# Correcting the diagonal block of the second attention by one addition of a skewed product, with four score banks

## What is computed

```
r     = sinusoid(S-1 ... 0, dk)                       # position vectors
term1 = einsum('bhqd,bhkd->bhqk', Q, K)
term2 = einsum('bhqd,kd->bhqk', Q, r)
term3 = einsum('hd,bhkd->bhk', u, K)
term4 = einsum('hd,kd->hk', v, r)
scores = (term1 + term3 + rel_shift(term2 + term4)) / sqrt(dk)
attn  = softmax(scores)
```

## Time and profile before

| | us |
|---|---|
| median of 3 timed runs | 2261.0 (2257.3 to 2263.5) |
| profiled execution | 2253.5 |
| its span, first to last instruction | 2251.5 |
| TensorE busy in the span | 1776.5 (79%) |
| VectorE busy | 1507.1 (67%) |
| ScalarE busy | 1508.9 (67%) |
| first attention | about 137 to 970 |
| mixing | about 980 to 1152 |
| second attention | about 1153 to 1905 |
| dense | about 1905 to 2251 |

### The profile page before, as it was taken

How to read it: one execution, slowest core, us unless ns; L and a number is a source line. 1 busy time by engine, 2 the same in 40 slices (tenths; PEclk the granted TensorE clock), 3 DMA queues, 4 the chain that set the end, 5 groups by cost and what they waited for, 6 DMA issues and landing times. The chain is left out here.

```text
span 2251.5 us, 44817 instructions
## 1 busy us (share of the span) xinstructions
PE 1776.5 (79%) x12182; PEld 1060.1 (47%) x12182; DVE 1507.1 (67%) x3898; ACT 1508.9 (67%) x2584; POOL 71.3 (3%) x102
## 2 busy tenths in 40 slices
PE   2407999999899989838628888888888885899998
PEld 1204555555555555525415444554454553444554
DVE  2636888888888888828848777777777774342431
ACT  2306888888888888828838788888778885222322
POOL 0000000000000000004400000000000000000000
PEclk9657999999999999969959999999999998899999
DMA  3947889889899889736852222222222221210000
GB/s 91 378 168 227 265 261 269 263 264 269 254 272 266 259 256 271 239 101 184 288 176 77 65 66 70 66 67 63 67 68 68 65 70 46 68 37 19 23 19 10
DMA packets 319461, 340.71 MB, mean 151 GB/s; under 512 B 24960, under 2 KB 241128, under 8 KB 319232
## 3 DMA queue, kind: packets, MB, share of 16 engines
q1 hardware_dynamic: 319360, 339.67, 49.7%
HBM read 193.23 MB, written 146.37 MB: 151 GB/s over the span
## 5 line engine op out<-in xcount | busy, mean ns | idle before, releaser
L750 ACT ACTIVATE a_prob<-bank,a_negmax 128x512 f32<-128x512 f32 x1024 | 712.8, 696 | 107.2 <-DVE a_negmax L695 97.2
L695 DVE TENSOR_REDUCE a_negmax<-bank 128x1 f32<-128x512 f32 x1024 | 700.0, 684 | 0.1
L757 ACT COPY a_probt<-bank 128x512 f32<-128x512 f32 x1024 | 597.9, 584 | 142.1 <-PE bank L587 128.8
L587 PE MATMUL bank<-a_ident,a_prob 128*128 128x128 f32 x4096 | 649.8, 282 | 34.8 <-ACT a_probt L757 31.2
L587 PEld LDWEIGHTS bank<-a_ident,a_prob 128*128 128x128 f32 x4096 | 439.5, 143 | 93.7 <-ACT a_probt L757 51.8
L672 DVE COPY_PREDICATED bank<-a_mask,bank 128x128 f32<-128x128 uint32 (+1 forms) x1024 | 290.0, 283 | 257.9 <-PE bank L572 169.5
L563 PE MATMUL bank<-a_stks 65*128 65x192 bf16 (+7 forms) x1024 | 327.9, 320 | 165.0 <-ACT a_prob L750 114.6
L563 PEld LDWEIGHTS bank<-a_stks 65*128 65x128 bf16 (+1 forms) x1024 | 100.1, 98 | 445.7 <-ACT a_prob L750 392.6
L600 PE MATMUL bank<-a_probt,a_vs 128*32 128x512 f32 x2048 | 275.5, 612 | 1.7 <-ACT a_probt L757 1.7
L569 PE MATMUL bank<-a_stks 96*128 96x128 bf16 (+2 forms) x1024 | 225.9, 221 | 33.6 <-DVE bank L672 23.3
L682 DVE TENSOR_TENSOR bank<-bank,a_band 128x192 f32<-128x192 f32 (+1 forms) x512 | 200.2, 391 | 59.1 <-DMA a_band<-shear_b 58.5
(11 more groups left out here) (165 smaller groups left out, 1541.8 us busy)
## 6 DMA issues: line engine op xcount, KB each, us to landing
a_band<-shear_b SPq DMA_DIRECT2D x128, 512.0 KB, 5.3
shear_a<-a_keyside SPq DMA_DIRECT2D x128, 256.0 KB, 4.5
a_sheared<-shear_a SPq DMA_DIRECT2D x128, 256.0 KB, 4.7
shear_b<-a_corr SPq DMA_DIRECT2D x128, 256.0 KB, 5.1
a_stks<-stack SPq DMA_DIRECT2D x128, 192.0 KB
a_stks<-stack SPq DMA_DIRECT2D x256, 96.0 KB
heads_out<-a_outs SPq DMA_DIRECT2D x64, 256.0 KB, 2.2
stack<-part SPq DMA_DIRECT2D x16, 768.0 KB, 5.2
```

The lines of the kernel that those rows point to most:

```text
L587: last = pe.transpose(turned_bank[k][:, n * 128:(n + 1) * 128], prob[h.slot % 2][:, n, k * 128:(k + 1) * 128], ident[:, :])
L695: v.tensor_reduce(negmax[h.slot % 2][:, n:n + 1], score[:, :], AX.X, ALU.max, negate=True).then_inc(maxed, 1)
L750: nc.scalar.activation(prob[h.slot % 2][:, n, :], score[:, :], ACT.Exp, bias=negmax[h.slot % 2][:, n:n + 1]).then_inc(exped, 1)
L757: nc.scalar.copy(probt[h.slot][:, k, :], turned_bank[k][:, :]).then_inc(copied, 1)
```

## The change

In the second attention the score tile is now cut at column 128n + 129: near product to the left, far product to the right, both into one of four score banks. The masked copies and their products go. Instead, what row q lacks from column q + 1 on inside the block (minus its own near product, plus the next query's product, and zero in column q + 1) depends on the column's distance to the diagonal alone, so it is a product of an unrotated query array with a fixed matrix of 96 rows and 128 columns (`edges`). TensorE makes it per head (`edge`), VectorE copies it out (`edge_out`), SyncE writes it to `shear_b` and reads it back skewed, as in the first attention, and `finish` adds it. Lookahead becomes 7 and 5 tiles. The stack gets a fifth array (the query with v, unrotated), which the mixing stage splits and writes too. The dense stage's code loses the parts that only layer 0 would have used; its instructions stay.

```diff
+KEY, EDGE, NEAR, FAR = range(4)
+ARRAYS = 5
-SCORE_AHEAD, EXP_AHEAD = 6, 4
+SCORE_AHEAD, EXP_AHEAD = {0: 6, 1: 7}, {0: 4, 1: 5}
...
-                score_banks = bank[0:4] if rel else bank[0:3]
-                others = bank[4:5] if rel else bank[3:5]
+                score_banks = bank[0:4]
+                other = bank[4]
-                key_bank, corr_bank = bank[5], bank[6]
+                key_bank, corr_bank = bank[5], bank[6] if rel else bank[4]
...
-                        sp.dma_start(stk[j][0:SR, KLO:QLO + 1, :], stack[1][b, :, own, 0:2, :]).then_inc(stk_in[j], 16)
-                        sp.dma_start(stk[j][0:SR, KHI, :], stack[1][b, :, own, 0, :]).then_inc(stk_in[j], 16)
-                        sp.dma_start(stk[j][0:SR, QHI, :], stack[1][b, :, own, 1, :]).then_inc(stk_in[j], 16)
-                        sp.dma_start(stk[j][SR:R1, QLO:QHI + 1, :], stack[1][b, :, own, 2:4, :]).then_inc(stk_in[j], 16)
+                        sp.dma_start(stk[j][0:SR, KEY:NEAR + 1, :], stack[1][b, :, own, 0:3, :]).then_inc(stk_in[j], 16)
+                        sp.dma_start(stk[j][0:SR, FAR, :], stack[1][b, :, own, 2, :]).then_inc(stk_in[j], 16)
+                        flat = stack[1][b, :, own, :, :].rearrange("j c a t -> j c (a t)")
+                        sp.dma_start(stk[j][SR:R1, EDGE, :], flat[:, :, T + 1:2 * T + 1]).then_inc(stk_in[j], 16)
+                        sp.dma_start(stk[j][SR:R1, NEAR:FAR + 1, :], stack[1][b, :, own, 3:5, :]).then_inc(stk_in[j], 16)
...
-                    if rel and left > 1:
+                    if left > 1:
                         hold(sp, added, 4 * (n + 1))
                         shear_b_read(sp, Head(i, j + 2))
-                    if rel and left > 2:
+                    if left > 2:
                         shear_b_write(sp, Head(i, j + 3))
...
                         for j in range(1 if rel else 0, LOAD_AHEAD):
                             head_load(sp, Head(0, j))
+                        if not rel:
+                            sp.wait_ge(edges_set, BASE + 3)
+                            sp.dma_start(edges[SR:R1, :], back[:, :]).then_inc(edge_in, 16)
+                            every = bass.AP(t["poskey"].tensor, 0, [[T, SR], [0, unroll], [1, T]])
+                            sp.dma_start(stks[SR:R1, :, KEY, :], every).then_inc(poskey_in, 16)
+                            for j in range(2):
+                                shear_b_write(sp, Head(0, j))
+                                shear_b_read(sp, Head(0, j))
+                            shear_b_write(sp, Head(0, 2))
...
+                    def edge(pe, h):
+
+                        pe.wait_ge(corr_copied, BASE + h.n)
+                        pe.wait_ge(stk_in[h.slot], BASE + per_stk * (h.i + 1))
+                        for n in range(NT):
+                            q = slice(128 * n, 128 * n + 128)
+                            last = pe.matmul(corr_bank[:, q], stk[h.slot][:, EDGE, q], edges[:, :], start=True, stop=True)
+                        last.then_inc(corr_mm, 1)
...
+                            if not rel and k == 1 and left >= CORR_AHEAD:
+                                edge(pe, Head(i, j + CORR_AHEAD))
...
                         if not rel:
+                            pe.wait_ge(edge_in, BASE + 48)
+                            for j in range(CORR_AHEAD):
+                                edge(pe, Head(0, j))
...
+                    def edge_out(v, h):
+                        v.wait_ge(corr_mm, BASE + h.n + 1)
+                        v.wait_ge(b_written, BASE + 16 * (h.n - 1))
+                        v.tensor_copy(corr[h.slot % 2][:, :, :], corr_bank[:, :].rearrange("p (n r) -> p n r", n=NT)).then_inc(corr_copied, 1)
...
+                                if left >= (k + score_ahead) // NT:
+                                    if rel:
+                                        mix(v, *ahead(i, j, k, score_ahead))
+                                    else:
+                                        finish(v, *ahead(i, j, k, score_ahead))
+                                if left >= (k + score_ahead - 1) // NT:
+                                    row_max(v, *ahead(i, j, k, score_ahead - 1))
...
+                                if not rel and k == 3 and left >= CORR_AHEAD:
+                                    edge_out(v, Head(i, j + CORR_AHEAD))
...
-                HALF = 2 * T
+                WIDE = 5 * T + 2
+                QV, KEYS, QU, ROT0, ROT1 = 0, T + 2, 2 * T + 2, 3 * T + 2, 4 * T + 2
+                HALVES = slice(0, ROT0), slice(ROT0, WIDE)
-                N_STACK = 4 * len(TERM_RUNS)
+                N_STACK = ARRAYS * len(TERM_RUNS)
```

More of the change, by code:

```diff
@@ L352, in attention_phase @@
                 ident = sb("ident", [128, 128])
-                mask = sb("mask", [128, 128], U32)
                 outs = sb("outs", [128, T])
+                wide = WIN if rel else REL
+                corr = [sb(f"corr{i}", [128, NT, REL]) for i in range(2)]
+                band = [sb(f"band{i}", [128, NT, wide]) for i in range(2)]
+                if not rel:
+                    edges, signs = sb("edges", [R1, REL], BF16), sb("signs", [SR, 2])
+                    waves, back = sb("waves", [SR, T], BF16), sb("back", [SR, REL], BF16)
                 if rel:
+                    mask = sb("mask", [128, 128], U32)
                     tabs = sb("tabs", [RF, unroll, 2 * REL], BF16)
@@ L709, in _ @@
                         else:
-                            for j in range(unroll):
-                                v.memset(stks[0:R1, j, KHI, :], 0.0).then_inc(blank, 1)
+                            v.memset(back[:, 0:1], 0.0).then_inc(edges_set, 1)
+                            v.wait_ge(edge_in, BASE + 32)
+                            v.tensor_copy(back[:, 1:REL], bass.AP(waves[:, :].tensor, T - 1, [[T, SR], [-1, REL - 1]])).then_inc(edges_set, 1)
+                            v.tensor_scalar(edges[0:SR, :], waves[:, 1:REL + 1], signs[:, 0:1], -1.0, ALU.mult, ALU.mult).then_inc(edges_set, 1)
@@ L721, in _ @@
+                        for n in range(score_ahead):
+                            if rel:
+                                mix(v, *ahead(0, 0, 0, n))
+                            if rel and n:
                                 row_max(v, *ahead(0, 0, 0, n - 1))
                             finish(v, *ahead(0, 0, 0, n))
+                            if not rel and n:
+                                row_max(v, *ahead(0, 0, 0, n - 1))
                         def vector_step(i, j, left):
                             for k in range(NT):
-                                if left >= (k + SCORE_AHEAD) // NT:
-                                    mix(v, *ahead(i, j, k, SCORE_AHEAD))
@@ L774, in _ @@
                                 corr_out(act, Head(0, j))
-                        for n in range(EXP_AHEAD):
+                        for n in range(exp_ahead):
                             exp_tile(act, *ahead(0, 0, 0, n))
@@ L1485, in gated_products, with flip @@
+                            last.then_inc(e["out_mm"], 1)
+                        def flip(b):
+                            pe.wait_ge(e["x1"], BASE + b + 1)
+                            for n in range(NT):
+                                last = pe.transpose(flip_bank[:, n * 128:(n + 1) * 128], x1n[:, n, :], ident[:, :])
+                            last.then_inc(e["tr1"], 1)
                         def gated_products(b):
@@ L1714, in step1, with step @@
-                        def step1(b, more, load):
+                            v.wait_ge(e["x1"], BASE + b + 1)
+                            v.tensor_copy(x1[:, :, :], x1n[:, :, :]).then_inc(e["kept"], 1)
+                            v.wait_ge(e["kept"], BASE + b + 1)
+                        def step(b, more, load):
                             for m in range(KH):
@@ L1726, in step1 @@
                                 keep_rows1(b + 1)
-                            rows2(b)
-                        if first:
-                            v.memset(xt1[:, 0:1], 0.0).then_inc(fill, 1)
-                            v.memset(vt[:, :, :, DH:VC], 1.0).then_inc(fill, 1)
-                            for i in range(3):
-                                v.memset(part[:, i, 4 * T:4 * T + 2], 0.0).then_inc(fill, 1)
-                            v.wait_ge(fill, BASE + 5)
+                            v.wait_ge(e["f_stored"], BASE + 16 * b)
+                            rows(v, b, pre2, x2, 2)
                         v.wait_ge(c_in, BASE + 16 * N_FIRST)
@@ L1740, in _ @@
                         keep_rows1(0)
-                        if first:
-                            token_mix(0)
-                            relu(0)
-                            residual2(0)
-                            rows2(0)
-                        steps(v, step0 if first else step1)
+                        steps(v, step)
         tables_phase()
@@ L1755, in build @@
         end_phase()
-        dense_phase(1)
+        dense_phase()
 def _tables(np):
```

450 lines of the change are left out of this document (127 added, 323 removed).

## The result

The changed kernel takes 2387.3 us (median of 4 runs, 2378.1 to 2392.3) against 2261.3 (2257.3 to 2263.5) for the kernel before: a ratio of 1.056, 95% interval 1.052 to 1.059. It is 126 us slower, and 104 us above the forecast. The profiled execution has a span of 2385.7 us against 2251.5, 134 us more.

The account below looks back on a forecast made before the run. SyncE's issues and the band's round trip were taken to bound the changed second attention. Loop -4, start +23, last heads -5 and mixing +12 gave +26 us, so 2283 us (base 2257), range 2238 to 2320.

Parts of the forecast that it names:

- the circle: Second attention's loop: band read landing, VectorE's steps, next write, loads, next read; two heads need L + 7.9, 5.78 us a head.
- L: Second attention: time for the 256 KB band read to land, taken as 3.0 us.
- the stall at the loop's edge: Second attention's 12-head loop: 0.38 us a head before; claimed to fall mostly into time VectorE waits anyway.
- SyncE becomes the bound and eats the gain: Second attention's loop: added DMA issues make it 5.70 us a head against 5.74, -4 us instead of 155 gained.
- SyncE alone 5.53: Second attention's loop: SyncE's issues alone take 5.53 us a head, 5.3 to 5.7 depending on the gap.
- rival (c): Second attention's loop: the circle binds harder, L = 3.6 or more, 6.0 to 6.1 us a head, about 2320 us; chance 0.13.
- Start +23: Start of the second attention: edge load stands behind seven heads' loads, first exponential 23 us later (18 to 28).
- Last heads -5: Last 16 heads, outside the second attention's loop: 81 us against 86, -5 (-12 to +3).
- Mixing +12: Mixing stage: splitting and writing a fifth array adds 12 us (8 to 20), 8.4 of it splitting.
- Rival (a): Second attention's loop: SyncE does not set the pace; ScalarE does, 4.7 us a head with leftovers, 2170 us; chance 0.15.
- Rival (d): Score banks, second attention: bank change does nothing since TensorE stays late; same time as forecast; chance within the forecast's 0.50.
- the signs named: Second attention's profile: SyncE hardly waiting for group output, VectorE waiting for most band reads, weighting products 5.5 to 5.8 us apart.

Follow-up runs that it names:

- early: Changed kernel with VectorE's band-product copy moved ahead of the band-read wait and TensorE's product one tile step earlier: 2340.2 us, 1.037 of the kernel before.
- pool: Changed kernel with the four stack loads of each head in the second attention issued by GpSimd instead of SyncE: 2318.6 us, 1.027 of the kernel before.
- unroll8: Changed kernel with 8 instead of 12 heads in the loop body of the second attention: 2353.6 us, 1.044 of the kernel before.
- shift: Changed kernel with 64 small semaphore instructions on SyncE in front of the second attention's loop, body unchanged: 2346.9 us, 1.038 of the kernel before.
- mix4: Changed kernel with four of five arrays stored in the mixing stage, splitting still over five, loads reading another array: 2325.3 us, 1.030 of the kernel before.
- noband: Changed kernel without the band product's store and read in the second attention's loop, compute kept: 2144.0 us, 0.950 of the kernel before.
- before_shift: Kernel before, with 64 small semaphore instructions on VectorE in front of the second attention's loop: 2221.8 us, 0.985 of the kernel before.
- nohold: Changed kernel without the 12 small semaphore instructions behind SyncE's waits in the second attention's loop body: 2375.4 us, 1.052 of the kernel before.
- load24: Changed kernel with the last of four stack loads reading arrays 2 and 3 instead of 3 and 4: 2380.7 us, 1.055 of the kernel before.
- pool_ring: `pool_early2` with four band-product buffers, a semaphore per scratch place, and SyncE's store ahead of the same step's read: 2297.5 us, 1.017 of the kernel before.
- pool_early2: Changed kernel with loads on GpSimd, band copy ahead of the band wait, TensorE's product right behind the first score tile: 2246.9 us, 0.996 of the kernel before.
- pool_ahead5: `pool_early2` with band product, copy and store one head earlier, four buffers, a semaphore per place, read before store: 2222.3 us, 0.988 of the kernel before.
- pool_actstore: `pool_ahead5` with the group store and the load of the next values issued by ScalarE instead of SyncE: 2167.4 us, 0.961 of the kernel before.

## Why the prediction was wrong, step by step

The loop was forecast at 5.70 us a head and takes 6.59. Two steps failed: the circle was priced too low, above all its landing time L (0.55 us a head, 57 us in 104 heads), and the stall at the loop's edge was put at nothing (0.34 a head, 35 us).

- **SyncE becomes the bound and eats the gain**: right, and the step on which the sign rested. Without the two DMAs a head the same compute runs at 4.49 us (forecast 4.3).
- **SyncE alone 5.53**: mis-sized, 5.80 by `early`. The loads take 0.2 more than the earlier trace rows showed, and once in four heads a gap is 0.3 longer. This doesn't show in after's total, since the circle covers it.
- **The circle**: right in form, wrong in one term; this is the larger miss. L was taken as 3.0, from the 3.6 of a read of twice the bytes. From the read to VectorE's start it was 3.0 to 4.3. With 3.7, 3.2 and 4.8 the formula gives (2 x 11.7 + 1.31) / 4 = 6.18 us; measured 6.25. So of the 0.55, L is 0.35; 0.08 is that the prediction took 5.70 although its own formula gave 5.78, without a reason; the rest are small terms. The price was rival (c)'s, "L = 3.6 or more", with 6.0 to 6.1. Moving the copy took 47 us away. What I had not seen is that the 4.7 us of loads covered the landing of the store, 3.2 us here and 4.0 in `pool`; so taking the loads away does not shorten the circle (`pool`).
- **"The loop-edge stall mostly falls into the time that VectorE waits anyway"**: this step failed too. It was priced at about zero and is 4.4 us a turn, 0.34 a head, 35 us in all (34 to 40 went with it in `unroll8` and `shift`). In the kernel before the stall sat on VectorE, which the new waits might have hidden; in the changed one SyncE, the bound itself, stops. The cause is a body's place in the program, which no operation of the change tells. With these two, 5.70 becomes 6.25 + 0.34 = 6.59.
- **Start +23**: first exponential +25. The first group store is 28 us later, 3 more; the band reads are 3.8 to 6.8 us apart there.
- **Last heads -5**: -1 for all that follows the 27th store. The last groups come 23.5, 20.5 and 17.9 us apart; the last seven heads, without loads, are at 4.5 to 5.1.
- **Mixing +12**: 15.0 us from the first stack write to the next stage (123.6 against 108.6), between the value taken and the bound of 20. By `mix4` the splitting cost 7.4 (forecast 8.4) and the stores 7.6 (forecast 4), with the DMA engines at 0.98 against 0.79 in `mix4`. The other 4.6 us lie ahead of it, where both kernels run the same code; over the other kernels with this mixing stage the first stack write came anywhere from 1039.0 to 1055.0.
- **Rival (a), 2170 us**: fell. Beside it stood the rule of the Trainium skill, "DMA: Bandwidth & Descriptors", section "Rules for kernel authors", that the fixed setup cost of a DMA overlaps with compute when it is issued early. It didn't decide here: the loads were issued seven heads ahead, and the queue still set the pace through the time of its issues, 5.80 us a head in `early`. It took four moves (loads to GpSimd, the product and its copy earlier, the store a head earlier, the group store to ScalarE) to reach 2167; that the rival's number was the same is chance.
- The estimate from the Trainium skill, "DMA: Bandwidth & Descriptors", section "Anatomy of one DMA" (L = 2.6 us), was too low: the profile of the changed kernel has this read at a median of 3.3 us.
- Rival (d): under SyncE's pace nothing shows of the fourth bank, as said. Whether (d) itself holds stays open: the fourth bank and the single addition were only run together (`noband`, 4.49 against 5.37 us a head).
- Of the signs named, SyncE's wait for the group output went and VectorE waits for the read in 45 of some 64 heads, but a head without an edge is at 6.25 us, above the 5.5 to 5.8 named.

By parts: the loop is 92 us above its forecast (+88 in place of -4), the start 5, what lies ahead of the second attention 7.5 and the end 4. That makes 108, and with the forecast's +26 the 134 us measured between the two profiled executions.

## What to carry to other kernels

A queue that has room is a resource like an engine: add up its issues, and then follow each round trip (store, landing, read, landing, compute, store) as a circle through all the waits that stand in line in that queue. If such a circle binds, break it with order first: make the product before the wait that it doesn't need, store it a head earlier, and keep waits for slow outputs out of the queue that feeds the bound. And before any comparison of two hardware loops look at the packets on the instruction queue and at the spacing across the loop's edge; a stall there may belong to the layout of the code and not to the change, and it can be 35 us on either side.

## What the runs showed of the hardware

- A loop body of 237 instructions on SyncE, or 303 on VectorE, cost 4.4 and 4.8 us a turn in one place of the program and nothing 64 instructions further on (`shift`, `before_shift`), with 28 to 30 against 0 to 3 packets on q14 in 420 us. A body of 225 on SyncE showed both (3.1 us in `nohold`, 4.3 in `load24`, none in `mix4`); 597 on TensorE showed none. That the packets are the body, fetched again, is the likely reading; which length and place decide was not settled.
- An issue of a stack load takes 0.70 us on SyncE ahead of the loop and 0.73 to 0.80 in it, 0.56 on GpSimd; of a 128-row transfer 0.36 to 0.39 on SyncE. From one load to the next it is 0.75 us on SyncE ahead of the loop, 0.93 to 1.0 in it, where addresses come from registers, and 0.67 on GpSimd.
- A 256 KB read landed in 3.7 us (median of 34) where a 256 KB store was issued some 0.7 us ahead of it (`pool_ring`), and in 3.5 (median of 58) where the store came behind it (`pool_early2`). With a group store and a load of values ahead as well it took 5.5 (18 reads) and 4.4 (19 reads).
- Idle time costs TensorE's clock. In the changed kernel TensorE stood idle for 3.39 us up to 1546.74, waiting in the end for a band read, and for 4.84 us up to 1557.74, behind an edge. The weighting that came next took 1.93 and 1.94 us, against 1.07 five us later and 1.06 in the earlier trace rows: the lower of the two levels, 1.2 in place of 2.4 GHz. The granted clock in 1280 to 1700 us was 0.89 in the changed kernel, 0.91 without its edge (`shift`), 0.98 in `pool_ahead5`, 0.99 and 1.00 where ScalarE set the pace (`pool_actstore`, `noband`), and 1.00 in `before_shift`.

```profile
1548.27 1.93 PE L610 MATMUL bank<-a_probt,a_vs 128*32 128x512 f32 x8 [0.22 <-ACT a_probt L796]
1559.26 1.94 PE L610 MATMUL bank<-a_probt,a_vs 128*32 128x512 f32 x8
1564.65 1.07 PE L610 MATMUL bank<-a_probt,a_vs 128*32 128x512 f32 x8
```
